# The last key's share of two cross-attentions, moved behind the output projection

## The reference

```
def _L2_xattn_ref(x, tab_x, tab_g, tab_b, vid_g, vid_b, Wq, Wk, Wv, q_g, q_b, k_g, k_b, Wo, bo):
    ...
    kv_in = layernorm(tab_x, tab_g, tab_b)
    q = layernorm(layernorm(x, vid_g, vid_b) @ Wq, q_g, q_b)
    k = layernorm(kv_in @ Wk, k_g, k_b)
    v = kv_in @ Wv
    ...
    sim = jnp.einsum('bhid,bhjd->bhij', q, k)
    attn = jax.nn.softmax(sim, axis=-1)
    out = jnp.einsum('bhij,bhjd->bhid', attn, v)
    ...
    return out @ Wo + bo

def _L3_xattn_ref(q, k, v, Wq, bq, Wk, bk, Wv, bv, Wo, bo):
    ...
    qh = _split_heads(q @ Wq.T + bq)
    kh = _split_heads(k @ Wk.T + bk)
    vh = _split_heads(v @ Wv.T + bv)
    score = jnp.einsum('bhqd,bhkd->bhqk', qh, kh) / jnp.sqrt(jnp.float32(D_K))
    attn = jax.nn.softmax(score, axis=-1)
    out = jnp.einsum('bhqk,bhkd->bhqd', attn, vh)
    ...
    return out @ Wo.T + bo
```

## Time and profile before

| | us |
|---|---|
| three runs | 3589.63, 3600.79 (median), 3603.87 |
| profiled execution: span from first to last instruction | 3592.7 |
| TensorE busy in it | 3255.0 (91%) |
| VectorE busy | 2199.0 (61%) |
| ScalarE busy | 1310.5 (36%) |
| GpSimd busy | 1145.0 (32%) |
| third cross-attention | about 1264 to 2011 |
| fourth cross-attention | about 2903 to 3297 |

### The profile page before, as it was taken

One profiled execution on the slowest core, in us unless ns is written; L12 is line 12 of the kernel. 1 busy time (PEld: TensorE's weight loads), 2 busy tenths in 40 slices (PEclk: granted clock), 3 DMA queues, 4 the chain that ended last, 5 costly groups with the idle time before them and its releaser, 6 DMA issues.

```text
span 3592.7 us, 94930 instructions
## 1 busy us (share of the span) xinstructions
PE 3255.0 (91%) x40134; PEld 2714.6 (76%) x40134; DVE 2199.0 (61%) x5259; ACT 1310.5 (36%) x3223; POOL 1145.0 (32%) x1809
## 2 busy tenths in 40 slices
PE   7989559979988889999999789979999999998996
PEld 5866457548975668888888567878888878887895
DVE  5757643456675166666666577744444458887557
ACT  5643101323221234444444443323222336665221
POOL 6767133121023343333333332300000035554103
PEclk9999779989998989999999899979999999999997
DMA  5620367631022321111111100012112111111000
GB/s 165 199 69 4 108 212 219 202 105 49 3 64 94 88 72 48 48 48 48 48 48 31 57 2 3 3 64 81 64 59 83 65 46 50 49 50 64 3 3 27
DMA packets 211334, 246.69 MB, mean 69 GB/s; under 512 B 19460, under 2 KB 191232, under 8 KB 207968
## 3 DMA queue, kind: packets, MB, share of 16 engines
q1 hardware_dynamic: 203424, 230.39, 20.1%
q0 software_dynamic: 7488, 10.23, 1.6%
HBM read 221.51 MB, written 18.61 MB: 67 GB/s over the span
## 4 chain that ended last, share of the span: by engine, by line
PE 74%; DVE 12%; issue 6%; POOL 3%; ACT 3%; DMA 1%; SPq 0%; ACTq 0%; POOLq 0%; DVEq 0%
PE psum L189 44%; PE psum L3671 11%; PE psum L983 2%; PE psum L3921 2%; PE psum L955 2%; PE psum L3130 2%; PE psum L3231 1%; PE psum L3199 1%; PE psum L3911 1%; PE psum L968 1%; DVE l2a_ss L1651 1%; DVE g_xn L258 1%; POOL l0a_ms L1183 1%; PE psum L3140 1%; DVE g_xn L1658 1%
## 5 line engine op out<-in xcount | busy, mean ns | idle before, releaser
L245 POOL TENSOR_SCALAR g_rs<-g_mv 128x4 f32<-128x4 f32 x24 | 5.1, 214 | 772.2 <-DVE g_mv L378 771.7
L3671 PE MATMUL psum<-l2f_hhi,l2f_whi 128*128 128x512 f32 x512 | 199.2, 389 | 0.0
L3671 PE MATMUL psum<-l2f_hlo,l2f_whi 128*128 128x512 f32 x512 | 199.2, 389 | 0.0
L3671 PE MATMUL psum<-l2f_hhi,l2f_wlo 128*128 128x512 f32 x512 | 199.2, 389 | 0.0
L189 PE MATMUL psum<-l2x_kT,l2x_Qp 128*128 128x257 f32 x768 | 179.2, 382 | 2.7 <-ACT g_xn L3554 2.6
L3725 DVE CAST l2f_hhi<-l2f_tmp 128x512 fp32r<-128x512 f32 x96 | 41.0, 427 | 201.4 <-ACT l2f_tmp L3788 200.3
L189 PEld LDWEIGHTS psum<-l2x_kT,l2x_Qp 128*128 128x128 f32 x768 | 141.9, 191 | 21.9 <-issue 3.2
L389 DVE TENSOR_TENSOR g_x<-g_x,psum 128x256 f32<-128x256 f32 x128 | 53.2, 416 | 136.0 <-PE psum L189 133.0
L3788 ACT ACTIVATE l2f_tmp<-psum,g_cols 128x512 f32<-128x512 f32 x64 | 44.2, 690 | 240.1 <-PE psum L3671 240.1
L3554 ACT ACTIVATE g_xn<-psum,l2x_sm 128x257 f32<-128x257 f32 x192 | 89.0, 473 | 90.8 <-DVE l2x_sm L3460 90.8
L4118 ACT ACTIVATE l3x_P<-psum,l3x_sm 128x257 f32<-128x257 f32 x256 | 117.8, 480 | 2.7 <-DVE l3x_sm L4040 2.4
(11 more groups left out here) (887 smaller groups left out, 10714.9 us busy)
## 6 DMA issues: line engine op xcount, KB each, us to landing
l2f_raw<-L2f_h SPq DMA_DIRECT2D x64, 512.0 KB, 3.2
l0f_w<-L0f_w SPq DMA_DIRECT2D x23, 1024.0 KB
l0x_ctxT<-ctxT SPq DMA_DIRECT2D x64, 257.0 KB, 2.8
l1x_ctxT<-ctxT SPq DMA_DIRECT2D x64, 257.0 KB, 6.0
l0x_ctok<-ctx SPq DMA_DIRECT2D x64, 256.0 KB, 3.2
l1x_ctok<-ctx SPq DMA_DIRECT2D x64, 256.0 KB
l2x_cT<-ctxT SPq DMA_DIRECT2D x64, 256.0 KB, 2.7
l2x_tok<-ctx SPq DMA_DIRECT2D x128, 128.0 KB, 2.9
```

The source lines that it names most:

```text
L3671: t = e.matmul(z, a, b, start=c == 0 and u == 0, stop=c == 7 and u == 2)
```

## The change

In both layers the last key no longer goes through the heads' banks. Its value rows are multiplied by the output weights once per layer and per head: VO, one row of 256 per batch and head. These rows are written to DRAM (768 rows in the third, 1024 in the fourth) and fetched per tile by four transfers into VO[128 x 256], triple buffered. The probabilities of the last key of four batches are gathered in ptl[128 x 32], transposed in 32 x 32 blocks on DVE, and spread with a mask into Rt[128 x 4 x 32], once per tile. Project begins with one matmul Rt x VO and adds the old ones to it. So per tile, in the third layer one transpose (line 3204) and 12 matmuls of 12 rows go, in the fourth four matmuls with VX go (and four VectorE transposes, four GpSimd spreads), and one matmul of 128 x 256 comes in each. The masks `rowmod` and `rowquad` have 128 rows.

The third layer, on TensorE (making the value rows, `tails_out`, turn_p and heads):

```diff
-                    for n in range(2):
-                        matmuls(e, take("vt", 0, n)[0:64, 0:384], [(tlT[:, c, :], wv[:, c, n * 384:(n + 1) * 384])
-                                                                   for c in range(2)]).then_inc(*vt_ps.up())
+                    z = take("vt", 0)
+                    for ch in range(6):
+                        t = matmuls(e, z[:, ch * 64:(ch + 1) * 64], [(wv[:, c, ch * 128:(ch + 1) * 128], tlT[:, c, :]) for c in range(2)])
+                    t.then_inc(*vt_ps.up())
...
+            def tails_out(k):
+                w.wait_ge(vtT_ok.at(1))
+                zz = [take("to", k, par) for par in range(2)]
+                for u in range(2):
+                    for par in range(2):
+                        r = slice(64 * par, 64 * par + 64)
+                        t = e.matmul(zz[par][0:64, u * 256:(u + 1) * 256], vtT[r, 2 * k + u, :], wo[r, 2 * k + u, :], start=True, stop=True)
+                t.then_inc(*to_ps.up())
             def spread0(b):
+                if 1 <= b < 4:
+                    tails_out(b - 1)
...
-                if b % 4 == 3:
-                    i = b // 4
-                    w.wait_ge(ptl_ok.at(b + 1))
-                    e.transpose(take("pl", i)[0:12, 0:128], ptl[i % 2][:].rearrange("p n j -> p (n j)"), ident[:]).then_inc(*pl_ps.up())
...
-                w.wait_ge(r_in[i % 2].at(3 * (i // 2 + 1)))
-                w.wait_ge(Rt_ok.at(i + 1))
...
-                for ch in range(6):
-                    for par in range(2):
-                        o, h, d = head(ch, par)
-                        t = e.matmul(o, VT[i % 2][:, d], Rt[:, h % 4], start=False, stop=True, skip_group_check=True)
```

The third layer's project:

```diff
+                w.wait_ge(Rt_ok.at(i + 1))
+                w.wait_ge(vo_in[i % 3].at(4 * (i // 3 + 1)))
+                e.matmul(z[:, 0:256], Rt[i % 2][:].rearrange("p j q -> p (j q)"), VO[i % 3][:], start=True, stop=False)
                 w.wait_ge(o_act.at(i + 1))
                 w.wait_ge(o_dve.at(i + 1))
-                matmuls(e, z[:, 0:256], [(oT[:, ch, :], wo[:, ch, :]) for ch in range(6)]).then_inc(*y_ps.up())
+                matmuls(e, z[:, 0:256], [(oT[:, ch, :], wo[:, ch, :]) for ch in range(6)], start=False).then_inc(*y_ps.up())
```

The third layer, on SyncE:

```diff
+                if b == 9:
+                    keep_tails()
+                if b % 4 == 3 and b >= 11:
+                    fetch_tails(b // 4 - 2)
```

The fourth layer, on TensorE, ahead of the ticks:

```diff
+            w.wait_ge(t_ok.at(2))
+            for m in range(2):
+                if m:
+                    w.wait_ge(to_ok.at(1))
+                for a in range(2):
+                    for r in range(4):
+                        p = slice(32 * r, 32 * r + 32)
+                        t = e.matmul(bank[r][0:64, a * 256:(a + 1) * 256], vtT[p, a, m, :], wo[p, m, :], start=True, stop=True)
+                t.then_inc(*to_ps.up())
+            w.wait_ge(to_ok.at(2))
```

The fourth layer's values, on TensorE:

```diff
-                w.wait_ge(r_in[q % 2].at(16 * (q // 2 + 1)))
-                w.wait_ge(Pt_ok.at(b + 1))
-                e.matmul(z[:, 0:128], VX[q % 2][:, b % 8, :], Pt[b % 2][:], start=True, stop=False, skip_group_check=True)
```

The fourth layer, on ScalarE, ahead of the ticks:

```diff
+            for m in range(2):
+                w.wait_ge(to_ps.at(m + 1))
+                copy_act(e, vto[:, m, :], K.big[0:64, 0:2048]).then_inc(*to_ok.up())
```

The fourth layer's turn, on VectorE:

```diff
-                w.wait_ge(ptl_ok.at(b + 1))
-                e.transpose(Pt[b % 2][:], ptl[b % 2][:]).then_inc(*Pt_ok.up())
...
+                if b % 4 == 3:
+                    i = b // 4
+                    w.wait_ge(tail_p.at(b + 1))
+                    if i >= 1:
+                        w.wait_ge(Rt_ok.at(i))
+                    e.transpose(ptT[:], ptl[i % 2][:]).then_inc(*pl_ok.up())
+                    w.wait_ge(pl_ok.now())
+                    if i >= 2:
+                        w.wait_ge(y_ps.at(i - 1))
+                    e.tensor_tensor(Rt[i % 2][:], ptT[:].unsqueeze(1).to_broadcast([128, 4, 32]),
+                                    rmod[:].unsqueeze(2).to_broadcast([128, 4, 32]), ALU.mult).then_inc(*Rt_ok.up())
```

The fourth layer, on SyncE:

```diff
-                if b % 8 == 3:
-                    rows(b // 8)
+                if b == 5:
+                    keep_tails()
+                if b % 4 == 3 and b >= 7:
+                    fetch_tails(b // 4 - 1)
+            fetch_tails(15)
```

More of the change, by code:

```diff
@@ L3057, in sp, with keep_tails, fetch_tails @@
             barrier(K, w)
[L3059 to L3066, removed]
+            kept = A["xs"][0:768, :]
+            def keep_tails():
+                w.wait_ge(to_ok.at(6))
+                load(e, vo_out, kept.rearrange("(b h) d -> b h d", h=12), vto.rearrange("b c a d -> b (c a) d"))
+            def fetch_tails(i):
+                w.wait_ge(vo_out.at(1))
+                w.wait_ge(zero.at(5))
+                if i >= 3:
+                    w.wait_ge(y_ps.at(i - 2))
+                src = kept.rearrange("(i j n h) d -> i h n j d", i=16, j=4, n=3)
+                for h in range(4):
+                    load(e, vo_in[i % 3], VO[i % 3][32 * h:32 * h + 12, :], src[i, h])
             for b in range(64):
@@ L3076, in sp @@
                          A["ctx"][b, 128 * kt:128 * kt + 128, :].rearrange("p (h s) -> p h s", h=2))
-                if b % 4 == 1 and b >= 5:
-                    rows(b // 4 - 1)
-            rows(15)
+                if b == 9:
+                    keep_tails()
+                if b % 4 == 3 and b >= 11:
+                    fetch_tails(b // 4 - 2)
+            for i in range(14, 16):
+                fetch_tails(i)
         def pe(e):
@@ L3260, in pool @@
             for c in range(2):
-                e.memset(VT[c][:], 0.0).then_inc(*zero.up())
+                e.memset(ptl[c][:], 0.0).then_inc(*zero.up())
+            for a in VO:
+                e.memset(a[:], 0.0).then_inc(*zero.up())
             w.wait_ge(ahead.c0_ok.at(0))
@@ L3945, in project @@
                 z = take("y", i)
+                w.wait_ge(Rt_ok.at(i + 1))
+                w.wait_ge(vo_in[i % 3].at(4 * (i // 3 + 1)))
+                e.matmul(z[:, 0:256], Rt[i % 2][:].rearrange("p j q -> p (j q)"), VO[i % 3][:], start=True, stop=False)
                 w.wait_ge(oT_ok.at(b + 1))
-                matmuls(e, z[:, 0:256], [(oT[i % 2][:, c, :], wo[:, c, :]) for c in range(2)]).then_inc(*y_ps.up())
+                matmuls(e, z[:, 0:256], [(oT[i % 2][:, c, :], wo[:, c, :]) for c in range(2)], start=False).then_inc(*y_ps.up())
             ticks(64, {1: keys, 2: scores, 4: turn, 5: values, 6: project}, order)
```

145 lines of the change are left out of this document (82 added, 63 removed).

## The result

| | before | after |
|---|---|---|
| median of four runs each | 3600.74 us | 3575.43 us |
| lowest and highest | 3589.63, 3603.87 | 3572.26, 3589.06 |
| ratio, 95% interval | | 0.9935 (0.991 to 0.9959) |
| span of the profiled execution | 3592.7 | 3587.3 |

A forecast was written before the change was run, and what follows sets the result against it. TensorE was taken to bound both loops, with ScalarE's chain close behind in the fourth. The third's -17.7 us and the fourth's +1.3 (-8.2 loop, +9.5 start) gave -16.4, from 3600.8 to 3584.4 us, range 3570 to 3602.

The forecast's parts named there:

- What bounds the kernel: Both loops: TensorE sets the time (74% of the span), so matmuls removed come back unless another chain stands close behind.
- Rival 4: Ticks losing matmuls are set by a chain beside TensorE, projection ticks by TensorE: +24.3 us, 3625.1; chance 0.04.
- Rival 5: VO comes late, so one wait is traded for another: gain some -8 us, 3593; chance 0.05.
- Third, last tile: Third's last project: the new matmul runs in the 0.75 us wait for oT, so -1.57 us.
- Third, start: Third's ticks 4 to 6: VO groups cost +1.8 us, the clock gives back -0.8; +1.0 in all.
- Fourth, loop: Fourth's ticks: plain ones -0.21 us each, down to 5.15, those with projection +0.12; -8.2 over 16 tiles.
- TensorE alone would give back 0.22 to 0.31 per tick: Fourth's ticks: TensorE's saving without the VX matmul, 0.22 to 0.31 us, limited to 0.21 by ScalarE's chain in plain ticks.
- Rival 1: Fourth's loop gives all that TensorE loses, -13.0 us: -21.2 in total, 3579.6; chance 0.17.
- rival 2: Fourth's plain ticks give nothing, as ScalarE's chain already sets them: -6.3 us in total, 3594.5; chance 0.15.
- Fourth, start: Before the fourth's first keys: products, copies, ctxhi and ctxlo 7.5 us, fallen clock +2.0; +9.5 in all.
- Rival 3: The clock does not fall at the fourth's start: -18.4 us in total, 3582.4; chance 0.09.
- Sum: Whole kernel: third stage -17.7 us plus fourth stage +1.3, -16.4 in total.

The follow-up runs named there:

- before_fill: Kernel before, with unread matmuls filling waits at the third's start and before its last projection; 61.83 us from first scores to first heads, instead of 62.25.
- thin_back: Changed kernel with VO's matmul last in the third's project and 12 thin matmuls back in the last tile; one run, last projection's clock did not fall.
- thin_out: Kernel before, without the 12 matmuls of 12 rows in the third's last tile; one run, 60.74 us from first scores to first heads.
- act_order: Changed kernel, with ScalarE copying ctxhi ahead of PT in the fourth; one run, plain tick 5.13 us, tick with projection 6.43.
- third_only: Kernel before with the change in the third cross-attention alone; ratio to before 0.9928 (0.9909 to 0.9947), -26 us.
- among_queries: Changed kernel with the fourth's VO products and copies moved among its query products; ratio to before 0.992 (0.9899 to 0.9941).
- the best version: Changed kernel with the fourth's VO products among its queries and ScalarE's ctxhi ahead of PT; 3565.29 us, ratio to before 0.9906 (0.9893 to 0.992).
- after_again: The changed kernel, unchanged, timed again beside the kernels with half the change; ratio to before 0.9949 (0.9929 to 0.997), -18 us.
- fourth_only: Kernel before with the change in the fourth cross-attention alone; ratio to before 1.0009 (0.9996 to 1.0021), +3 us.

## Why the prediction was right, point by point

- **What bounds the kernel**: right. Time taken off TensorE's stream in the third came back in full, -17.2 against -17.1. The wait chain of the heads' tick moved with it, and the price of the new matmul, 0.43, is the measured one. Rivals 4 and 5 are out: the heads' tick got shorter, and no wait for VO stands at project.
- **Third, last tile**: -3.1 instead of -1.6. The sized part is right: `before_fill`, which keeps the thin matmuls but fills the wait, has 11.68 us there, after has 10.14, so 1.54 are theirs. The rest is the clock, 1.6 us, which the prediction left out though it could be read: 4.51 us in the earlier trace rows, where 12 times the 0.215 of the earlier trace rows are 2.6. It is no sure gain: both traces of the old third as it was lost it, `thin_back` with the same wait and thin matmuls did not.
- **Third, start**: -1.5 in the trace of after (-1.0 and -0.5), where +1.0 stood. The clock makes the difference. Up to the first scores the new third takes 23.7 us in the five traces with a granted clock of 1.00 there, and 25.3 in the four with 0.93 (28.5 in one with 0.82); the kernel before took 24.67 with 0.93. At like clock this stretch, which holds the group of tick 4, costs about 0.6 us more, and the -1.0 is luck. The groups of ticks 5 and 6 stand behind the first scores. `thin_out` has the old start with the clock held, and takes 60.74 us from there to the first heads: these two cost 61.7 - 60.74 = 1.0 us net (each is 1.01 long, the one in tick 5 goes into the wait). Together that is about 1.6, where 1.8 was forecast. Against it stand 1.5 us of clock (62.25 - 60.74), where half of 1.66 was counted.
- **Fourth, loop**: -6.8 instead of -8.2. The plain tick is right to the hundredth, 5.15, but half by luck. The failed step is "TensorE alone would give back 0.22 to 0.31 per tick", and its use of the 0.31 in the tick with projection. In the trace before, the VX matmul began 0.12 us behind the matmul ahead of it (2947.55, 2947.67), and its follower 0.31 behind it (2947.98). Without it the values begin 0.21 behind the last keys' matmul (3180.45 to 3180.66): the 0.09 of changing to the small matmuls is paid by whoever stands ahead of them. So TensorE gives back 0.22, just what ScalarE's slack of 0.21 allowed, and the tick with projection pays -0.22 + 0.43 = +0.21, not +0.12: 16 x 0.09 = 1.4 us. Rival 1 (all of 0.31) could not have come even with ScalarE out of the way, as the 5.13 of `act_order` shows; rival 2 (plain ticks of 5.36) is out.
- **Fourth, start**: +10.55 instead of +9.5. The copies are 1.87 us each against 1.85 taken between 1.4 and 2.3 from the rows. The Trainium skill (ScalarE: Activation LUTs, What ACT_TABLE_LOAD costs) made it 1.89 by an estimate from its price per element, and the trace agrees. ctxhi and ctxlo are 2.02 against 2.03. The mis-sized terms: one half is 1.09 us, not 0.69, because the scores' row that it was taken from writes to both halves of the output partitions and these products to one half only (that this is the reason was not tried); and the clock cost 0.89 in the second half beside 1.48 in the keys, 2.4 in all against 2.0. The sum 7.5 + 0.8 + 2.4 is 10.7. The clock's part is of this execution: with the same matmuls from keys to scores, the traces with this start took 4.3 to 5.1 us there instead of 3.07. The Trainium skill (TensorE: Matmul & The Clock Gate, What's actually happening) says that an idle TensorE falls back to 1.2 GHz; here the granted clock was 0.50 behind the waits in every kernel with this start. Rival 3 is out.
- **Sum**: the stages of the change moved by -17 to -18 us (with or without the stretch up to the third's first scores), -16.4 forecast. The third gave 4.1 us more than forecast, 3.9 of them by the clock (1.6 in the last tile, 0.7 behind the first scores, 1.6 ahead of them), and the fourth 2.5 less. The two errors cancel in part, so the total is better than its parts, and that is luck. The runs as a whole gained more than their stages in four cases (23 us against 17 to 18, 26 against 21 in `third_only`, 29 against 26 in `among_queries`, 34 against 27 in the best version) and about the same in two (`after_again` and `fourth_only`); only the interval of the best version leaves its stages out. The four kernels with the old third took 893.5 to 897.8 us for the unchanged code between third and fourth, nine of the ten with the new one 883.3 to 891.7, and after 898.6. Whether the change reaches into that code, by the clock or otherwise, was not tried; with one trace per kernel it stays open.

## What to carry to other kernels

Work that is made once per layer has a price that depends on where it stands: the same products and copies cost 10.5 us in front of an empty pipeline and 2.3 us among matmuls that were running anyway. When an instruction is taken out of a busy engine's stream, count the distance between the starts of its neighbours without it, not its own distance to its follower, which can contain a changeover that stays. And when two chains end together, read both before naming the bound: taking work off either alone gave 0.02 us per tick here at most, off both 0.27.

## What the hardware showed beyond that

A halved clock cost this kernel 1.6 to 1.7 us behind a wait of 0.75 us in two of the three executions that had thin matmuls ahead of it, and nothing in the two that had none. At the fourth's start, behind waits of 1.99 and about 4 us, the granted clock was 0.50 in all eight executions that have these waits. Spans of unchanged code differed by up to 15 us between executions (883.3 to 898.6 between third and fourth), with a mean granted clock of 0.89 to 0.94 in the layer that made most of it. So a trace of a change of this size is compared by stages, from landmark to landmark, and each stage with the granted clock beside it: the third's loop agreed within 0.2 us among the traces that share it, and the fourth's within 0.8, where whole runs of one kernel lie 9 to 25 us apart.
